# Shifted cross attention of a four-layer network: one query stack in place of two, a pair's heads interleaved on the trip through memory

## The reference

```python
ph = (pe @ w_p).reshape(2 * s, N_HEADS, D_K).transpose(1, 0, 2)   # positions
ac = jnp.einsum('bhtd,bhsd->bhts', qh + b_u[None, :, None, :], kh)
bd = jnp.einsum('bhtd,hmd->bhtm', qh + b_v[None, :, None, :], ph)
bd = left_shift(bd)          # row i is read i places further left
scores = (ac + bd) / math.sqrt(D_K)
scores = jnp.where(mask[:, None, :, :], scores, jnp.float32(-jnp.inf))
attn = jax.nn.softmax(scores, axis=-1)
```

## Time and profile before

| | us |
|---|---|
| median of 3 runs (2083.02 to 2091.57) | 2091.0 |
| the profiled execution, its own time | 2087.96 |
| its span, first to last instruction | 2086.2 |
| L0_ffn ends and L1_attn begins | about 240 to 353 |
| L1_xattn, first shift to last heads | about 684 to 985 |

### The profile page before, as it was taken

How to read it: one execution, slowest core, us unless ns; L and a number is a source line. 1 busy time by engine, 2 the same in 40 slices (tenths; PEclk the granted TensorE clock), 3 DMA queues, 4 the chain that set the end, 5 groups by cost and what they waited for, 6 DMA issues and landing times.

```text
span 2086.2 us, 39703 instructions
## 1 busy us (share of the span) xinstructions
PE 1720.5 (82%) x14024; PEld 1311.1 (63%) x14024; DVE 1455.4 (70%) x5662; ACT 1035.3 (50%) x2588; POOL 461.5 (22%) x448
## 2 busy tenths in 40 slices
PE   6588999999998678879998687899868868765886
PEld 5455687776776445546887465555548856554775
DVE  6689524777877578778888777778875466567643
ACT  3277525666765556656333354456434435531343
POOL 3300110000002000000556200000364544213442
PEclk9899999999999789989999799899979989976998
DMA  5334067000001978885200333323125543242356
GB/s 179 79 75 115 16 243 230 1 1 1 1 1 31 280 214 233 250 215 165 81 1 19 94 76 90 76 65 96 47 73 182 165 132 93 71 147 79 97 163 203
DMA packets 211053, 228.54 MB, mean 110 GB/s; under 512 B 16052, under 2 KB 179276, under 8 KB 210216
## 3 DMA queue, kind: packets, MB, share of 16 engines
q1 hardware_dynamic: 205864, 215.71, 36.1%
q0 software_dynamic: 4992, 10.30, 1.4%
HBM read 130.57 MB, written 94.98 MB: 108 GB/s over the span
## 4 chain that ended last, share of the span: by engine, by line
PE 47%; DVE 26%; DMA 9%; ACT 7%; issue 4%; POOL 3%; SPq 2%; another core or an unknown queue 1%; DVEq 0%; ACTq 0%; POOLq 0%
PE banks L746 40%; ACT P L1509 4%; DVE P L1993 4%; PE banks L1059 3%; DMA stacks<-region 2%; DMA back<-mask,block_to 2%; DVE region L1915 2%; SPq L2684 2%; DVE P L1835 2%; DVE route L1835 1%; DVE P L2092 1%; DVE region L2162 1%; PE banks L1151 1%; ACT region L1509 1%; DVE skew_room L1835 1%
## 5 line engine op out<-in xcount | busy, mean ns | idle before, releaser
L2508 POOL TENSOR_TENSOR norms<-norms,consts 128x2 f32<-128x2 f32 x112 | 81.5, 728 | 1224.5 <-DVE norms L1839 1223.9
L1509 ACT ACTIVATE P<-P,negm 128x256 f32<-128x256 f32 x512 | 240.5, 499 | 109.2 <-DVE negm L2112 64.6
L1509 ACT ACTIVATE P<-banks 128x512 f32<-128x512 f32 (+2 forms) x392 | 188.4, 511 | 162.5 <-PE banks L746 155.2
L1509 ACT ACTIVATE region<-banks 128x384 f32<-128x384 f32 (+4 forms) x221 | 108.5, 506 | 80.7 <-PE banks L746 58.8
L746 PE MATMUL banks<-xnT,region 128*128 128x256 f32 x544 | 139.3, 390 | 3.4 <-ACT xnT L1509 3.3
L746 PE MATMUL banks<-kz,qs 128*128 128x256 bf16 (+1 forms) x512 | 112.0, 280 | 34.8 <-DVE negm L1993 14.2
L746 PE MATMUL banks<-region 64*128 64x256 f32 (+6 forms) x922 | 126.7, 364 | 8.9 <-ACT region L1509 3.5
L746 PE MATMUL banks<-qv,region 128*128 128x256 bf16 (+2 forms) x512 | 117.6, 270 | 18.2 <-ACT P L1509 13.7
L746 PE MATMUL banks<-qs,kz 128*128 128x256 bf16 (+2 forms) x512 | 117.1, 270 | 16.7 <-ACT P L1509 8.2
L746 PE MATMUL banks<-kz,region 128*128 128x256 f32 x512 | 121.7, 384 | 4.0 <-DVE skew_room L1835 2.8
L2587 POOL DMA_INDIRECT back<-mask,block_to x92 | 89.6, 974 | 111.7 <-DVE mask L2340 100.7
(11 more groups left out here) (292 smaller groups left out, 4465.4 us busy)
## 6 DMA issues: line engine op xcount, KB each, us to landing
stacks<-region SPq DMA_DIRECT2D x178, 192.0 KB, 3.0
sorted<-qs SPq DMA_DIRECT2D x4, 4160.0 KB
skew<-region SPq DMA_DIRECT2D x64, 256.0 KB
qs<-stacks SPq DMA_DIRECT2D x24, 384.0 KB
kz<-stacks SPq DMA_DIRECT2D x48, 192.0 KB
skew<-region SPq DMA_DIRECT2D x64, 128.0 KB
skew_room<-skew SPq DMA_DIRECT2D x32, 256.0 KB
P<-skew SPq DMA_DIRECT2D x32, 256.0 KB
```

What stands on the lines that cost most here:

```text
L1509: return a.e.activation(o, i, f, **kw)
L2508: g.e.tensor_tensor(room[:, :, 0], room[:, :, 0], pows[:, :], ALU.pow).then_inc(done, 1)
```

## The change

- `qv`, its drain, its pieces, its stack and its transfer back are gone. PE's `shift` takes `qs`. That leaves the difference b_v - b_u against the positions, one number for each head and position: a product of PE with `place` (`gap_of_heads`, once, in L0_attn of stream 0's last item), cut into three bf16 pieces (`gap_cut`), sent to memory and back into three rows of `phz` behind its 96. Against them stand three rows of ones in `qs` and `qv`, which DVE writes once per stream, in `L1_attn` of item 12 (3 * ITEMS), with a wait of its own.
- Layer 1's cross attention now alternates between the rooms `qs` and `qv`; q_back no longer waits for the item before, k_back still does. DVE, SP and POOL lose the steps of the old stack; where a turn would be missing, an empty `yield` keeps `TURNS` in step.
- ACT writes a pair's two heads interleaved, element by element (a pitch of 8 bytes), the rooms in memory have the same form, and DVE's `add_and_max` reads every other element. A packet becomes a row of both heads, 1024 or 2048 bytes; the bytes and the number of DMAs stay.

```diff
-        self.skewed = [skew_room[:, :, :, :], self.P[:, :, 1, :, :]]
+        self.skewed = [a.rearrange("p t k c -> p t (k c)") for a in (skew_room[:, :, :, :], self.P[:, :, 1, :, :])]
...
-        self.skew = nc.dram_tensor(f"skew{n}", (2, 2, S, 2 * S), F32).ap()
+        self.skew = nc.dram_tensor(f"skew{n}", (2, S, 2 * 2 * S), F32).ap()
...
+    shift_rooms = [[r.rearrange("p h t c -> p (h t c)").rearrange("p (t c h) -> p t c h", t=TOK, h=2) for r in pair] for pair in staging]
...
-        s.qs_of = {n: [s.qs[:, :, :], s.qs[:, :, :] if n == 4 else s.qv[:, :, :]] for n in FRONTS}
+        s.qs_of = {n: [s.qs[:, :, :], s.qv[:, :, :]] for n in FRONTS}
...
+            if (s.n, j) == (0, 3):
+                p.wait_ge(tables, GAP)
+                p.wait_ge(scalar_tables, PLACE)
+                mm(s.T[0:H, 0:S], gap_of_heads, place).then_inc(first_full, 1)
+                p.free[s.n, "T"] = (tables, GAP_CUT)
...
-            qs, qv, kz, v = s.qs_of[4][j % 2], s.qv_of[j % 2], s.kz_of[4][j % 2], s.v_of[4][j % 2]
+            qs, kz, v = s.qs_of[4][j % 2], s.kz_of[4][j % 2], s.v_of[4][j % 2]
...
+            p.wait_ge(place_sem, 96)
...
-                    i = mm(s.S1[:, t * S + far:(t + 1) * S], qv[:, h // 2, t * 128:(t + 1) * 128], phz[:, h % 2, h // 2, far:])
+                    i = mm(s.S1[:, t * S + far:(t + 1) * S], qs[:, h // 2, t * 128:(t + 1) * 128], phz[:, h % 2, h // 2, far:])
...
-                    p.wait_ge(s.stack_in, back_before(j) + 64)
+                    p.wait_ge(s.stack_in, back_before(j) + 48)
...
-                    a.wait_ge(s.stack_out, 32 * (stacks_before(j) + stacks_of(j) - 1))
+                    a.wait_ge(s.stack_out, 32 * (stacks_before(j) + 1))
...
-                    act(flat2(staging[s.n][h // 2 % 2][:, h % 2, :, :])[:, 128:], s.S1[:, 128:]).then_inc(s.shift_out, 1)
+                    act(shift_rooms[s.n][h // 2 % 2].rearrange("p t c h -> p (t c) h")[:, 128:, h % 2], s.S1[:, 128:]).then_inc(s.shift_out, 1)
...
-            v.wait_ge(s.stack_out, 32 * (stacks_before(j) + n_before))
+            v.wait_ge(s.stack_out, 32 * stacks_before(j))
...
-                if bv is not None:
-                    q_drained(bank, bv, s.natural_qv)
                 q_drained(bank, bq, s.natural_q).then_inc(s.q_out, 1)
-                if bv is not None:
-                    yield from q_pieces(s, j, s.natural_qv, 0)
-                yield from q_pieces(s, j, s.natural_q, 0 if bv is None else 1)
+                yield from q_pieces(s, j, s.natural_q)
+                if j // ITEMS == 4:
+                    yield
...
+                step(red(gap_of_heads.rearrange("p (a i) -> p a i", a=2), ident.rearrange("p (a d i) -> p a i d", a=2, d=DH), ALU.add))
+                step(tt(gap, P["L1x_vb"], P["L1x_ub"], ALU.subtract))
+                ts(gap_of_heads, gap_of_heads, gap, DH ** -0.5, ALU.mult, ALU.mult).then_inc(tables, 1)
...
+            if (s.n, j) == (0, 3):
+                v.wait_ge(first_full, GAP_FULL)
+                T = s.T[0:H, 0:S]
+                step(v.e.tensor_copy(gap_cut[:, 0, :], T))
+                step(tt(gap_rest, T, gap_cut[:, 0, :], ALU.subtract))
+                step(v.e.tensor_copy(gap_cut[:, 1, :], gap_rest))
+                tt(gap_cut[:, 2, :], gap_rest, gap_cut[:, 1, :], ALU.subtract).then_inc(tables, 1)
...
+            v.wait_ge(place_sem, 80)
+            if j == 3 * ITEMS:
+                v.wait_ge(skew_zero, 224)
+                for room in s.qs_of[4]:
+                    i = v.e.memset(room[AUG:AUG + 3], 1.0)
+                i.then_inc(s.rooms_clean, 1)
             yield from k_of_quarter(0)
...
-                    yield from add_and_max(s, now, s.S0, lambda t: s.skewed[now // 2 % 2][:, now % 2, t, :], now % 2)
+                    yield from add_and_max(s, now, s.S0, lambda t: s.skewed[now // 2 % 2][:, t, :].rearrange("p (c h) -> p c h", h=2)[:, :, now % 2], now % 2)
...
-                g.wait_ge(skew_zero, 288)
+                g.wait_ge(skew_zero, 224)
...
-                    i = g.e.memset(room[:, :, 0, 128:], 0.0)
+                    i = g.e.memset(room[:, 0, S:], 0.0)
...
-                g.e.memset(s.qv_of[1], 0.0)
                 clean_v(s.v_of[4][1]).then_inc(s.rooms_clean, 1)
...
-            d.wait_ge(skew_zero, 160 if j < 2 * ITEMS else 288)
+            d.wait_ge(skew_zero, 96 if j < 2 * ITEMS else 224)
...
-            yield from stack_back(s, j, 0, [qs[0:AUG]] + ([qs[AUG:AUG + 6]] if j // ITEMS in (6, 7, 9) else []), 0)
+            yield from stack_back(s, j, 0, [qs[0:AUG]] + ([qs[AUG:AUG + 6]] if j // ITEMS in (6, 7, 9) else []),
+                                  ONES_BEHIND if j // ITEMS == 4 else 0)
...
-                d.wait_ge(place_sem, 64)
-                yield from stack_out(s, j, 2)
-                yield from stack_back(s, j, 2, [s.qv_of[j % 2][0:AUG]], ROOMS[4][1] if j % 2 else 0)
                 yield from stack_out(s, j, 0)
+                yield from q_back(s, j)
+                yield
                 yield from stack_out(s, j, 1)
                 yield
                 d.wait_ge(s.heads_out, H * (ITEMS + k))
                 d.wait_ge(s.stack_in, back_before(j) + 16)
-                yield from q_back(s, j)
+                yield
                 yield from k_back(s, j)
...
-            for k in range(4):
-                dma(s.skew[k // 2, k % 2, :, S:2 * S].rearrange("(t p) m -> p t m", p=128), zeros, skew_zero)
+            for k in range(2):
+                dma(s.skew[k, :, 2 * S:4 * S].rearrange("(t p) m -> p t m", p=128), zeros, skew_zero)
...
             if (s.n, j) == (1, 2 * ITEMS):
                 yield
+                d.wait_ge(tables, GAP_CUT)
+                d.wait_ge(place_sem, 64)
+                gap_rows = streams[0].via[2, 0:3 * H * S]
+                dma(gap_rows.rearrange("(k h s) -> h k s", k=3, s=S), gap_cut, place_sem)
                 d.wait_ge(rel_out_sem, 16)
                 for z in streams:
                     d.wait_ge(z.x_done, j)
@@ -2810,6 +2835,8 @@
                             n = rows.stop - rows.start
                             dma(copy.rearrange("(p k r) d -> p k r d", k=16, r=4)[rows],
                                 z.empty_rows[128 - n:].unsqueeze(1).to_broadcast([n, 16, 4, SORTED_W]), skew_zero)
+                d.wait_ge(place_sem, 80)
+                dma(phz[AUG:AUG + 3].rearrange("p a i s -> p (a i s)"), gap_rows.rearrange("(k m) -> k m", k=3), place_sem)
             yield
 
...
-                        dma(s.skew[slot, :, t * 128:(t + 1) * 128, far:S].rearrange("h p m -> p h m"), staging[s.n][slot][:, :, t, far:],
-                            s.lane_out[slot])
+                        dma(s.skew[slot, t * 128:(t + 1) * 128, 2 * far:2 * S],
+                            shift_rooms[s.n][slot][:, t, far:, :].rearrange("p c h -> p (c h)"), s.lane_out[slot])
...
-                        back = bass.AP(tensor=s.skew.tensor, offset=slot * 2 * S * 2 * S + t * 128 * (2 * S - 1) + S - 1,
-                                       ap=[[2 * S - 1, 128], [S * 2 * S, 2], [1, near]])
-                        dma(s.skewed[slot][:, :, t, 0:near], back, s.lane_in[slot])
+                        back = bass.AP(tensor=s.skew.tensor, offset=2 * (slot * S * 2 * S + t * 128 * (2 * S - 1) + S - 1),
+                                       ap=[[2 * (2 * S - 1), 128], [1, 2 * near]])
+                        dma(s.skewed[slot][:, t, 0:2 * near], back, s.lane_in[slot])
```

More of the change, by code:

```diff
@@ L436, in __init__ @@
         self.natural_k = self.picks[:, :, :, :].rearrange("p k t c -> p (k t c)").bitcast(F32)
-        self.natural_qv = self.mask[:, :, :].rearrange("p t c -> p (t c)").bitcast(F32)
         self.pick_w = sb("pick_w", [2, TOK])
@@ L607, in program @@
     place_cut = early_rooms[:, at_place + S:at_place + S + COMBOS * S // 2].bitcast(BF16).rearrange("p (n c) -> p n c", c=S)
-    assert at_place + S + COMBOS * S // 2 <= 8 * TOK * S
+    at_gap = at_place + S + COMBOS * S // 2
+    gap_cut = early_rooms[0:H, at_gap:at_gap + 3 * S // 2].bitcast(BF16).rearrange("p (k c) -> p k c", c=S)
+    gap_rest, place_rest = place[0:H], early_rooms[:, at_gap + 3 * S // 2:at_gap + 5 * S // 2]
+    assert at_gap + 5 * S // 2 <= 8 * TOK * S
+    at_heads = at_second + 2 * TOK * D
+    gap_of_heads, gap = region1[:, at_heads:at_heads + H], region1[:, at_heads + H:at_heads + H + 1]
+    assert at_heads + H + 1 <= 3 * E * F
     ones_t = sbuf("ones_t", [128, 128])
@@ L633, in program @@
               6: room(region2, free2 + 4 * head_size, n, v_size)}
-        s.qv_of = [s.qv[:, :, :], as_heads(room(region2, free2 + 2 * v_size, n, head_size))]
         pieces = {1: room(region1, at_rest, n, piece_size), 4: room(region2, free2 + 2 * v_size + 2 * head_size, n, piece_size),
@@ L663, in program @@
         nc.alloc_semaphore(n) for n in ("tables", "scalar_tables", "first_full", "constants"))
-    ROW_CUT, IDENTB, SIGNS, TWOS, MASK, PLACE_CUT, PADMAX = range(1, 8)
```

(16 more changed lines are left out.)

19 lines of the change are left out of this document (8 added, 11 removed).

## The result

The changed kernel takes 2128.8 us (median of 4 runs, 2126.2 to 2131.3), the kernel before 2087.0 beside it (median of 4, 2076.3 to 2091.6): a ratio of 1.0208, 95% interval 1.0179 to 1.0237, some 42 us slower. The profiled execution's span is 2129.2 us against 2086.2, so 43.0.

The account below looks back on a forecast made before the run. No engine was taken as the only bound; in the cross attention DVE bounds half an item's period, trips and start-up the other. The sum 43.1 + 3 + 2.5 - 20 - 10 = +18.6 us gave 2109 us against 2091.0, range 2082 to 2132.

Parts of the forecast that it names:

- The wait: Start of L1_attn: DVE's memsets wait for the fills of the sorted tokens' rooms, so PE stands 43.1 us (42 to 45).
- The memset: Rows of ones at the start of L1_attn: each DVE memset of 2048 elements takes 1.8 us, between 1.22 and 2.5.
- The clock: After PE's stand in L1_attn: its clock must come back, costing 3 us (up to 4, or none).
- The small additions: Seven small DVE instructions in L0_attn, 2 us, and stream 1's two memsets, 0.5 us (0 to 3.6): together 2.5 us.
- (a): Layer 1's cross attention: removing 23.4 us of DVE's work on the second query's mask, drain and cut gains 20 us.
- (b): Layer 1's cross attention: 44 us less transfer time gains 10 us (3 to 20), 6 for kz and 4 for shorter trips.
- (c): Layer 1's cross attention: accesses at a pitch of 8 bytes cost nothing; at double time, 108 us more DVE work.
- the sign that I had set for being wrong: PE has other work in the stand, fills land earlier, or the cross attention gives under 12 or over 38 us.
- the gain covers the stand: Rival: the cross attention gives 38 to 59 us, covering PE's wait for the fills; 2090 us, chance 0.22.
- full DVE: Rival: the cross attention becomes full on DVE throughout and faster, a gain of 73 us; 2067 us, chance 0.09.
- the pitch costs: Rival: pitched accesses in the cross attention add 108 us of DVE work, half on the path; 2163 us, chance 0.06.
- the harmless wait: Rival: the fills are in by 312, so PE loses nothing at the start of L1_attn; 2064 us, chance 0.03.

Follow-up runs that it names:

- e2: The kernel before plus only DVE's wait for the fills, ahead of layer 1's self-attention, no memset: 2125.4 us, ratio 1.0207.
- e5: The changed kernel with its rows of ones written by POOL behind the norms of a stream's fourth, last item of L1_attn: 2085.4 us, ratio 0.9975.
- e9: e6 without PE's product of the identity and the mask in the shifted cross attention, so the output differs: 2067.0 us, ratio 0.996 to the kernel before.
- e7: e6 plus 23.6 us of dummy subtractions on DVE where the second query's cut was: 2088.2 us, ratio 0.9987 to the kernel before.
- e6: e5 with the old trip (heads apart, ACT and DVE contiguous), keeping the one query stack and gap rows: 2080.9 us, ratio 0.9959 to the kernel before.
- e4: The kernel before with the interleaved trip alone, two query stacks kept and no rows of ones: 2089.2 us, ratio 1.0032.
- e10: e6 with trip rows of only 16 elements, unsheared, same number of transfers, so the output differs: 2065.0 us, ratio 0.9946 to the kernel before.
- e8: e6 with ACT alone writing at the pitch of 8 bytes, so the output differs: 2084.6 us, ratio 0.9971 to the kernel before.
- e11: The kernel before with the trip's transfers interleaved but ACT's write and DVE's read contiguous, so the terms are mixed: 2077.8 us, ratio 1.0023.
- e1: The changed kernel with its rows of ones written by POOL behind the norms of each stream's second item of L1_attn: 2124.1 us, ratio 1.0208.

## Why the forecast was right in sign and short in size

**The wait.** Forecast: DVE reaches it at 296.9, leaves at 351.3, and PE stands 43.1 us from 312.3. It reached it at 299.6 and the memset began at 354.75, 2.7 and 3.4 us later, most of it the lateness of 2.6 us that the kernel has from its start; PE stood 44.13. Shown twice over: e2 reproduces it with the wait alone, e5 removes it. The fills' landing, read off the fall of the DMA share in the earlier trace rows as 351.3, was right to 0.1 us: in e2, whose start isn't late, DVE goes on at 351.39.

**The memset** took 1.76 us for 3 x 2048 elements; I had taken 1.8 between 1.22 and 2.5. The Trainium skill, "VectorE: DVE Perf Modes", section "Zero memsets can be issued as uint32 (trn2)", gave an estimated 2.1; the row is a sixth under it.

**The clock.** Forecast 3. Lateness at the stand went up by 46.0 with 44.1 of standing, so 1.9.

**The small additions.** This is the first term that was mis-sized. I gave stream 1's two memsets 0.5 us (0 to 3.6), "where DVE has room". They cost 4.1: they lie ahead of a copy for PE's next scores, PE stood 2.60 us for it and ran 5 us at a clock of 0.70. The early additions cost 2.6 in after and 0.2 to 2.8 over the kernels that have them (forecast 2).

**(a) DVE's work on `mask`.** Forecast -20; this step failed. I scaled 23.4 us by the share of the stage in which DVE is full. The sum also mixed two stretches: the 23.4 us are of 665 to 985, the 301 of 684 to 985, in which only 16.2 of them lie. That isn't what decided. DVE full in 740:760 didn't mean that the stage waits for DVE there throughout. The chain of waits between two items points at what was right behind it. In before (start us, us, what) one stretch of it is the stack of the query with b_u on its way out (the second of the two to be cut, from `OT`), with ACT's copies for the cut of `k` behind it:

```profile
755.79 0.58 SPq L2684
756.37 0.04 issue
756.41 4.73 DMA stacks<-region
...
761.22 1.22 ACT region L1509 x2
```

In after, at the same place (some 52 us on), PE's own products and its turning of the weights (L1159) have taken the chain:

```profile
805.01 1.09 PE banks L1159 x4
806.09 1.20 PE banks L749 x16
...
807.96 1.10 PE banks L913 x8
809.06 1.44 PE banks L749 x20
```

Two stretches of chain are a pointer and no proof, and e9 doesn't bear out that PE's products are the bound. What measures the term is e7: 23.6 us of work put back are worth 5.8 us (3.5 by the landmarks). The rest went into DVE's waits for ACT and PE.

**(b) Transfers.** Forecast -10, of it 6 for `kz` and 4 for shorter trips. The second stack and its share of `kz` give about 3 (8.6 of e6 less 5.8 of e7; the interval of e7 takes in 0), PE's wait for `kz` being 7.9 us for 10.7. The trips gave nothing and took 3 to 7. The sum of 44 us less transfer time was too much in one half. By stretch, from 640 to the stage's end, in before, e6 (stack gone), e4 (interleaved alone) and after:

```profile
640.00:985.00 345.00, 263.98 (x2163) 187.25 (x2162) 262.12 (x913) 207.43 (x493) 21.96 (x24) 0.89 0.75 210
```

```profile
641.00:978.00 337.00, 260.29 (x2164) 184.97 (x2163) 242.20 (x875) 207.55 (x494) 18.48 (x22) 0.90 0.70 196
```

```profile
640.00:992.00 352.00, 266.57 (x2160) 188.03 (x2160) 261.69 (x913) 209.47 (x494) 22.09 (x24) 0.88 0.71 205
```

```profile
692.70:1033.00 340.30, 261.60 (x2163) 185.62 (x2162) 242.48 (x874) 209.54 (x493) 18.30 (x22) 0.89 0.66 194
```

Share times length is 259, 236, 250 and 225 us: the stack took 23 away (forecast 21), half the packets only 9 (forecast 24), both together 34. And that time is not what a trip waits for: a way takes 4.2 us, of which 2.4 to 2.5 pass before the first landing, and with half the packets it is no shorter. e10 shows how little even the bytes are worth.

**(c) The pitch.** DVE's 420 ns stayed 420, as the Trainium skill's "SBUF — State Buffer", section "Door 1: The DMA port swizzle", has it. ACT's write did not stay, and there the measurement goes against that rule: 511 ns for 481, 128 times, 3.8 us of ACT's work, for which I had said nothing. What of interleaving's 3 to 7 us is this and what the later landings stays open: e8 and e11 each give some of it by the ratio and little by the landmarks.

**The sum.** 44.1 + 1.9 + 6.7 - 4.9 is 47.8 where I had 18.6; the end of the program gave 4 to 5 back by itself. Of the 29 us of difference 25 are (a) and (b), 4 the small additions. By the sign that I had set for being wrong (the cross attention gives under 12 us) the second half of the forecast was wrong: it gave 4.9. That 2128.8 lies within 2082 to 2132 all the same is owed to the width that the rivals gave the range. It is 0.8 above the likeliest's own 2102 to 2128, the loss of 42 us is over twice the 18.6 of the sum, and no rival described a stand with next to no gain behind it. The rivals "the gain covers the stand" and "full DVE" fell with (a); "the pitch costs" was right in kind for ACT and far off in size; the harmless wait, made true in e5, gives 0.9975 and not the 0.987 that my 2064 stood for. What bounds the stage isn't settled: neither 23 us of DVE work, nor 29 us of PE's products, nor half of the transfer time moves it by more than 8 us. I take it for a loop through all of them, with each a little ahead of the next; no run takes two of them away together, so this isn't shown.

## What to carry to other kernels

A row of constants is cheap and its wait is not: before an instruction is given a wait, look at what is queued behind it on that engine, and when the awaited transfer lands, and do the same at the new place if it is moved (e1 cost as much as the change itself). Removed work is worth its share only while no other chain lies just behind; put the same work back in as a dummy and see what it costs before believing a proportion. A lower share of the DMA engines need not mean a shorter trip: measure from issue to landing.
